# Moving the last outputs and the last division of the second attention into the experts' program

## The reference, cut to what matters

```
q, k, v = heads(x @ Wq), heads(x @ Wk), heads(x @ Wv)      # 16 heads of width 16
attn    = softmax(causal(q k^T / sqrt(16)))
s       = (attn v) @ Wo + bo
h1, h3  = x @ W1[e].T, x @ W3[e].T                         # 16 experts of 176, one shared of 352
y       = sum_e (silu(h1) * h3 * combine[:, e]) @ W2[e].T  + shared expert
x       = x + s * silu(y)
```

## Time and profile before

| | |
|---|---|
| time, median of 3 runs (lowest to highest) | 866.46 us (866.29 to 870.01) |
| time of the profiled execution | 866.14 us |
| its span, first to last instruction | 864.4 us |
| TensorE busy | 757.0 us, 88% |
| VectorE busy | 523.5 us, 61% |
| ScalarE busy | 431.6 us, 50% |
| GpSimd busy | 430.2 us, 50% |
| mean granted clock of TensorE | 0.928 of full speed |

### The profile page before, as it was taken

One profiled execution on the slowest core, in us unless ns is written; L12 is line 12 of the kernel. 1 busy time (PEld: TensorE's weight loads), 2 busy tenths in 40 slices (PEclk: granted clock), 3 DMA queues, 4 the chain that ended last, 5 costly groups with the idle time before them and its releaser, 6 DMA issues. The chain is left out here.

```text
span 864.4 us, 12823 instructions
## 1 busy us (share of the span) xinstructions
PE 757.0 (88%) x3664; PEld 366.7 (42%) x3664; DVE 523.5 (61%) x1345; ACT 431.6 (50%) x922; POOL 430.2 (50%) x751
## 2 busy tenths in 40 slices
PE   3938999999999999954984789999569999999995
PEld 2322222223222222212752223332148888888884
DVE  3649777777777777323553877785035555555555
ACT  1431566656666655742132166776524455455552
POOL 1751556664234323421222123334277999799994
PEclk9985999999999999985997699999869999999997
DMA  5393740110020011012049362433221222122121
GB/s 183 122 295 92 160 90 15 38 47 13 20 61 18 15 45 39 20 39 67 0 148 290 88 186 68 127 98 95 66 79 48 61 61 68 51 64 71 61 64 56
DMA packets 60076, 69.84 MB, mean 81 GB/s; under 512 B 14905, under 2 KB 40858, under 8 KB 60011
## 3 DMA queue, kind: packets, MB, share of 16 engines
q1 hardware_dynamic: 60016, 69.15, 28.4%
HBM read 47.35 MB, written 15.47 MB: 73 GB/s over the span
## 5 line engine op out<-in xcount | busy, mean ns | idle before, releaser
L696 ACT ACTIVATE top<-ps 128x512 f32<-128x512 f32 (+3 forms) x384 | 171.0, 490 | 133.4 <-PE ps L643 133.3
L643 PE MATMUL ps<-mid 99*128 99x512 bf16 (+3 forms) x576 | 184.1, 335 | 8.2 <-ACT mid L696 5.0
L626 PE MATMUL ps<-mid 96*128 96x512 bf16 (+3 forms) x512 | 173.2, 360 | 15.5 <-PEq L231 11.1
L738 DVE CUSTOM_DVE_ANT_0 ps<-ps,keep 128x512 f32<-128x512 f32 (+3 forms) x320 | 161.7, 529 | 27.4 <-PE ps L626 26.8
L1479 PE MATMUL ps<-xp,wp 128*128 128x512 f32 (+1 forms) x600 | 149.3, 399 | 16.6 <-ACT wp L1531 8.7
L663 PE MATMUL ps<-top,mid 128*33 128x512 f32 (+3 forms) x768 | 161.8, 500 | 0.0
L1479 PEld LDWEIGHTS ps<-xp,wp 128*128 128x128 f32 (+1 forms) x600 | 114.6, 192 | 42.5 <-ACT xp L1533 9.1
L643 PEld LDWEIGHTS ps<-mid 99*128 99x128 bf16 x576 | 53.9, 98 | 180.8 <-ACT top L696 102.9
L820 POOL TENSOR_SCALAR_AFFINE_SELECT top<-top 128x128 f32<-128x128 f32 x256 | 71.2, 291 | 110.5 <-ACT top L696 108.1
L696 ACT ACTIVATE mid<-ps 128x512 f32<-128x512 f32 (+1 forms) x192 | 82.1, 493 | 65.1 <-PE ps L643 42.4
L742 DVE TENSOR_REDUCE top<-ps 128x1 f32<-128x512 f32 x128 | 88.2, 689 | 36.5 <-PE ps L626 35.8
(11 more groups left out here) (204 smaller groups left out, 815.5 us busy)
## 6 DMA issues: line engine op xcount, KB each, us to landing
mid<-part_scratch SPq DMA_DIRECT2D x9, 1152.0 KB, 8.8
part_scratch<-top SPq DMA_DIRECT2D x18, 384.0 KB, 5.3
top<-in_w SPq DMA_DIRECT2D x16, 396.0 KB, 3.9
cw_s<-combine_rows SPq DMA_DIRECT2D x48, 128.0 KB, 3.0
part_scratch<-top SPq DMA_DIRECT2D x18, 256.0 KB, 5.2
mid<-part_scratch SPq DMA_DIRECT2D x9, 384.0 KB, 3.9
top<-inverse_scratch SPq DMA_DIRECT2D x12, 256.0 KB
top<-in_w SPq DMA_DIRECT2D x8, 384.0 KB, 5.1
```

The source lines that it names most:

```text
L626: nc.tensor.matmul(ps[:, s_bank(turn), 0:w], queries(pair, m)[0:PARTS, i * P:(i + 1) * P], keys(pair, m)[0:PARTS, c * 512:c * 512 + w], st ...
L643: nc.tensor.matmul(ps[:, ST_BANK + n % AHEAD, 0:w], keys(pair, m)[0:STACK, j * P:(j + 1) * P], queries(pair, m)[0:STACK, q0:q0 + w], start ...
L696: nc.scalar.activation(pr[:, n % RING, 0:w], ps[:, ST_BANK + n % AHEAD, 0:w], ACT.Exp, scale=0.25).then_inc(p_ready, 1)
L738: ins = nc.vector.tensor_tensor_reduce(bank, bank, msk[:, 512 - w:512], -1.0 if low else 1.0, 3e38 if low else -3e38, ALU.add, ALU.min if ...
```

## The change: what it does

- SP sends the last 8 output DMAs (pair 7, c = 1) in the experts' block, behind the first `combine_weights`, no longer in attention's. The last piece of `w2s` is loaded before the inverses of c = 0.
- In SP's list of the experts, `combine_weights(2)` now stands before `last_inverses`.
- On VectorE, `last_inverted` moves behind unit 1, the low part of the tokens' second half comes over from GpSimd behind unit 2, and `last_scaled` (three instructions) comes over from GpSimd behind unit 3.
- On TensorE, all four parts of `through_wo` stand at units 22 and 23, two at each, with their `summed` on VectorE there too.

The diff, cut to its core:

```diff
-            def scale(pool, f, c):
+            def scale(eng, f, c):
...
-                    nc.gpsimd.tensor_tensor(to, to, repeated(c)[0], ALU.mult).then_inc(scaled, 1)
+                    eng.tensor_tensor(to, to, repeated(c)[0], ALU.mult).then_inc(scaled, 1)
...
+            def last_outputs(sp):
+                outputs(sp, N - 1, 1)
...
-                        inverses(sp, LASTF, 0)
-                        outputs(sp, N - 1, 1)
                         if not first:
                             sp.dma_start(w2s[0:NI - (GI - 1) * P, GI - 1, :], w2[(GI - 1) * P:NI, :]).then_inc(ld_m, 16)
+                        inverses(sp, LASTF, 0)
+                        if first:
+                            outputs(sp, N - 1, 1)
                         sp.wait_ge(landed, 48 * N)
...
                 combine_weights(0)
+                env["last_outputs"](sp)
                 combine_weights(1)
...
+                combine_weights(2)
                 env["last_inverses"](sp)
-                for n in range(2, UNITS):
+                for n in range(3, UNITS):
                     combine_weights(n)
...
-                    if c == 0 and isinstance(i, int) and 3 <= i < 4:
+                    if c == 0 and isinstance(i, int) and GI - 3 <= i < GI - 1:
                         for q in range(2):
-                            through_wo(q)
-                    if c == 0 and isinstance(i, int) and i >= GI - 3 and i < GI - 1:
-                        through_wo(2 + i - (GI - 3))
+                            through_wo(2 * (i - (GI - 3)) + q)
...
-                env["last_scaled"](pool)
-                pool.wait_ge(xh_ok, 2)
-                nc.gpsimd.tensor_tensor(xp[:, 1, :, 512:T], xT[:, :, 512:T], xp[:, 0, :, 512:T].bitcast(F32),
-                                        ALU.subtract).then_inc(xl2_ok, 1)
...
-                env["last_inverted"](dve)
+                def late_work(i):
+
+                    if i == 1:
+                        env["last_inverted"](dve)
+                    if i == 3:
+                        env["last_scaled"](dve)
+                    if i == 2:
+                        dve.wait_ge(xh_ok, 2)
+                        nc.vector.tensor_tensor(xp[:, 1, :, 512:T], xT[:, :, 512:T], xp[:, 0, :, 512:T].bitcast(F32),
+                                                ALU.subtract).then_inc(xl2_ok, 1)
...
+                    if c == 0 and isinstance(i, int) and i < 4:
+                        late_work(i)
-                    if c == 0 and isinstance(i, int) and i in (3, GI - 1):
+                    if c == 0 and isinstance(i, int) and i in (GI - 3, GI - 2):
                         for q in range(2):
-                            summed(q if i == 3 else 2 + q)
+                            summed(2 * (i - (GI - 3)) + q)
```

More of the change, by code:

```diff
@@ L479, in inverted @@
                 nc.vector.reciprocal(cd[:, c, 0, :], cd[:, c, 0, :]).then_inc(inv, 1)
-            def scale(pool, f, c):
+            def scale(eng, f, c):
                 to = o1[:, f, columns(c)]
-                pool.wait_ge(outs[c], PER[c] * 4 * (f + 1))
+                eng.wait_ge(outs[c], PER[c] * 4 * (f + 1))
                 if not first and c == 1:
-                    nc.gpsimd.tensor_tensor(to, to, second(f), ALU.add).then_inc(num_sum, 1)
-                    pool.wait_ge(num_sum, f + 1)
-                pool.wait_ge(inv_r[c], READS * (f + 1))
+                    eng.tensor_tensor(to, to, second(f), ALU.add).then_inc(num_sum, 1)
+                    eng.wait_ge(num_sum, f + 1)
+                eng.wait_ge(inv_r[c], READS * (f + 1))
                 if first:
                     n1, rd = second(f)[:, c, :], repeated(c)
-                    nc.gpsimd.tensor_tensor(n1, n1, rd[1], ALU.mult)
-                    nc.gpsimd.tensor_tensor(to, to, rd[0], ALU.mult).then_inc(scaled, 1)
+                    eng.tensor_tensor(n1, n1, rd[1], ALU.mult)
+                    eng.tensor_tensor(to, to, rd[0], ALU.mult).then_inc(scaled, 1)
                 else:
-                    nc.gpsimd.tensor_tensor(to, to, repeated(c)[0], ALU.mult).then_inc(scaled, 1)
+                    eng.tensor_tensor(to, to, repeated(c)[0], ALU.mult).then_inc(scaled, 1)
             def combine(dve, f, c):
@@ L511, in last_combined, with last_scaled @@
                 combine(dve, LASTF, c)
-            def last_scaled(pool):
-                scale(pool, LASTF, 0)
-                scale(pool, LASTF, 1)
+            def last_scaled(eng):
+                scale(eng, LASTF, 0)
+                scale(eng, LASTF, 1)
             with ExitStack() as b:
@@ L893, in _ @@
                                 inverses(sp, f - 1, 1)
-                        inverses(sp, LASTF, 0)
-                        outputs(sp, N - 1, 1)
                         if not first:
                             sp.dma_start(w2s[0:NI - (GI - 1) * P, GI - 1, :], w2[(GI - 1) * P:NI, :]).then_inc(ld_m, 16)
+                        inverses(sp, LASTF, 0)
+                        if first:
+                            outputs(sp, N - 1, 1)
                         sp.wait_ge(landed, 48 * N)
             here[1] = kept
-            return o1, combined, last_inverses, last_inverted, last_scaled, last_combined
+            return o1, combined, last_inverses, last_inverted, last_scaled, last_combined, last_outputs
         tmp[1] = 0
@@ L920, in late0 @@
                 far_maps0(sp, pair + 1)
-        o0, combined0, last_inverses0, last_inverted0, last_scaled0, last_combined0 = attention(
+        o0, combined0, last_inverses0, last_inverted0, last_scaled0, last_combined0, _ = attention(
             0, stack0, v0, 16, loaded0, late0)
@@ L958, in late1 @@
                 far_maps1(sp, (3, 1)[pair])
-        o1, combined1, last_inverses, last_inverted, last_scaled, _ = attention(
+        o1, combined1, last_inverses, last_inverted, last_scaled, _, last_outputs = attention(
             1, stack1, v1, 8, loaded1, late1)
```

## The result

| | before | changed |
|---|---|---|
| median (lowest to highest), 6 runs each | 867.21 us (865.10 to 870.01) | 855.43 us (850.91 to 856.46) |
| profiled execution, its span | 866.14, 864.4 us | 850.91, 849.2 us |
| mean granted clock | 0.928 | 0.936 |

The account below looks back on a forecast made before the run. TensorE was taken as the bound once units run, with SP's barrier and GpSimd's chain delaying unit 2. 866.14 - 13.2 - 2.8 + 3.7 = 853.9 us, 854.2 against the median; range 850.0 to 858.0.

Parts of the forecast that it names:

- Term 1: Barrier ahead of the experts: with SP's output DMAs moved behind it, the experts begin 5.63 us earlier.
- Term 2: Units 0 to 2 on TensorE: unit 2 starts at 629.3 instead of 642.49, 13.2 us gained, barrier's 5.6 included.
- `g` of unit 0 waits for GpSimd's weight part: VectorE ahead of unit 2: `g` could start at 628.35 but starts at 628.6 and ends at 629.3.
- Term 3: TensorE's clock in unit 2: full instead of low, 2.72 us instead of 5.49, 2.77 us gained.
- Term 4: VectorE and GpSimd taking turns: stalls of 0.6 us ahead of unit 5 and 3.1 ahead of unit 6, 3.7 lost.
- My list: Engine schedule from 629.3 us: `g` of unit 3 ends at 642.1, last division runs 642.8 to 647.2 between GpSimd's parts.
- my sign of 2 to 4 us of idle time ahead of unit 6: TensorE gap ended by `g` of unit 4, with VectorE's line 494 spread over 4.4 us around GpSimd's parts.
- the late weights of unit 3: `cw_s`, issued by SP behind the last inverses, arrives at 640.4 to 643; the upper case adds 1 us.
- Term 5: `through_wo` on TensorE: 16 products leave unit 3 (3.45 us) and stand at units 22 and 23; nothing gained or lost.
- rival 1: VectorE's late work is hidden, so term 4 is 0: 850.5 us, or 849.3 with an earlier clock; chance 0.22.
- Rival 2: Clock falls in the new gap ahead of unit 6, costing up to 2.77 us: say 857 us; chance 0.22.
- Rivals 3 and 4: 3: barrier not SP's alone, 859.8 us, chance 0.05; 4: turn-taking lengthens every unit's period, kernel slower, chance 0.02.

Follow-up runs that it names:

- the outputs alone: The kernel before with only the eight last output DMAs moved behind the barrier and the w2s load ahead of the inverses; 864.63 us, ratio 0.9967.
- the late work only: The changed kernel with the eight output DMAs back ahead of the barrier; 859.71 us, ratio 0.9903.
- the spread version: The changed kernel with unit 3's weights first, VectorE's division, inversion and low part spread over units 0 to 3 and 22; 852.64 us, ratio 0.9819.
- filler: Unused TensorE products at the experts' head: eight on the changed kernel, 855.96 us (0.9872); four on the kernel with spread VectorE work, 851.24 us (0.9805).

## Why the prediction was right, and where it was off

The prediction was 854.2 us and the measurement 855.43. That they are so close is partly luck: the terms below come to 14.5 us where I had 12.3, and the first series' medians differ by 11.8 us, the least of the three. By its terms, in the changed kernel's profile:

- **Term 1, the barrier.** Predicted 5.63 us, with 0.47 us from the last engine to the entry. It is 5.82 (6.10 - 0.28). The run with the outputs alone shows that the entry's 5.8 us don't reach unit 2 without term 2: that kernel gains 2.9 us, by other steps.
- **Term 2, unit 2.** From the copy's end it moved from 23.3 to 9.7 us: 13.6, predicted 13.2. The step "`g` of unit 0 waits for GpSimd's weight part" is there (0.96 in place of 0.69 us).
- **Term 3, the clock.** Row against row it is 5.49 - 2.98 = 2.51 us, predicted 2.77. The mechanism is right; I had set 5.49, the row of a unit behind a gap, against 2.72, that of a unit without one.
- **Term 4, what is late next.** Predicted 0.6 + 3.1 = 3.7 us, measured 0.56 + 1.07 = 1.6. The mechanism is right and the size was off. My list had `g` of unit 3 at 641.45, held by GpSimd's part, and GpSimd's next parts between all three instructions of the division, over 4.4 us. It took 3.0 us, and my sign of 2 to 4 us of idle time ahead of unit 6 did not come. I had also put the late weights of unit 3 down as up to 1 us more. They were late, by 1.2 to 1.4 us in three profiles, and did the opposite: GpSimd worked off its part meanwhile. With that wait gone, the gap is 2.58 us, close to my 3.1, and the division takes 4.6 us, as in my list. It is the same in the run of the late work only, where the wait was 0.87 us and the gap 2.57. But unit 5 is then not late at all: of my 0.6 us ahead of it the turns alone give nothing, and that 0.56 us was measured is luck, for it needs the late weights. So the wrong step is the order of turns behind a wait that I had counted as a plain addition.
- **Term 5, `through_wo`.** It moved and cost nothing: at units 22 and 23 it runs without a gap (TensorE is full from 719 to 734 us). No run moves it alone.
- **The sum.** 13.6 + 2.5 - 1.6 = 14.5 us, and from the copy the profiles have 13.8 to 14.7; predicted 12.3.

The rivals: rival 1 (no stall) is not what happened, but the spread version shows that it can be had. Rival 2 (the clock falls in the gap) did not happen in the three profiles of the changed kernel, whose gaps are 1.1 us; it did in three variants with gaps of 2.57, 2.58 and 3.7 us, and it didn't in one of 1.78. Rivals 3 and 4 are out: the entry is 0.28 us behind the copy, and from unit 7 on TensorE has no gap.

The Trainium skill's sentence (SBUF — State Buffer, Who interferes with whom) on two SBUF inputs and a GpSimd instruction that reads held in each of these profiles: VectorE's 512 columns took 0.68 us beside an idle GpSimd and up to 1.8 us beside a busy one, and GpSimd's own part grew from 1.3 to between 1.6 and 2.1 us. Of the five instructions that the prediction says the change brings to VectorE, four came over; line 477 was VectorE's before.

Two things stay open. One is why attention's end itself moves by up to 10 us from one execution to the next; it is ahead of everything that was changed. The other is what decides whether and when the clock falls at the entry; between the profiles of this entry without filler, unit 2 moves with it from 9.1 to 10.7 us after the copy.

## What to carry to other kernels

A wait ahead of a barrier and a chain behind it can hide each other. Move both, or measure first which one the next engine really follows: here the outputs alone gave 0.3% and the late work 1.0%, both together 1.5 to 1.8%. When work is handed to another engine's spare time, don't count its busy share but the slack of the one result that is waited for, and hand over one instruction per period rather than three in one (here 1.3 to 1.8 us by the profiles, which the runs alone don't set apart from noise). And a wait that goes can cost time, if another engine used it to get out of the way.

## What the runs showed of the hardware that was not expected

- TensorE's clock fell to 1.2 GHz in a gap of 3.7 us between units, and 1.2 and 0.7 us behind gaps of 2.57 and 2.58 us; it stayed up with gaps of 1.1 and 1.8 us. One fall made the next unit 1.5 to 2.5 us longer (4.3 to 5.3 us in place of 2.8). The length of the gap is not all of it: at the entry, behind 2.73 us of idle time each time, the clock fell in eight profiles, from 0.4 us ahead of unit 0 to 2.3 us into it, and stayed up in one.
- A call of `matmul` with float32 operands and 256 columns shows as two products on TensorE, 0.43 us together at full clock (16 rows for 8 calls, 3.45 us from the earlier trace rows); a call with float32r operands and 512 columns shows as one of 0.23 us (12 rows and 12 calls in a unit, 2.72 us). I had priced the filler at half of what it takes.
- The entry of a block followed the last engine by 0.28 us when that was ScalarE, and by 0.47 us when it was SP.
